# Query weights of later head pairs written between the key matrix' evictions, and the second norm's rows spread by a product with ones

## What is computed

```python
xn = layernorm(ctx, ln1_w, ln1_b)                 # 4 x 77 x 256
ln = layernorm(layernorm(x), ln2_w, ln2_b)        # 4 x 1024 x 256
q, (k, v) = ln @ Wq, split(xn @ Wkv)              # 16 heads of 64
q = q * (1 + f) + f                               # per batch and head
x = x + softmax(q k^T / 8) v @ Wout
y = layernorm(x)
x = x + top2_of_9_experts(y)                      # silu(y Wg) * (y Wu) @ Wd, weighted by the router
```

## Time and profile before

| | us |
|---|---|
| median of 3 runs | 809.99 (809.43 to 810.35) |
| the profiled execution's own time | 810.75 |
| its span, first to last instruction | 809.0 |
| PE busy in the span | 781.2 (97%) |
| DVE, ACT, POOL busy | 662.2, 622.3, 386.2 |
| mean granted TensorE clock | 0.989 |

### The profile page before, as it was taken

The page is one execution under the profiler, slowest core; times in us unless marked ns, Lnnn a source line. Parts: engine busy times, 40 slices in busy tenths (PEclk is TensorE's granted clock), DMA queues, the critical chain, the costliest instruction groups (busy, mean ns, idle before and its releaser), DMA issues.

```text
span 809.0 us, 19727 instructions
## 1 busy us (share of the span) xinstructions
PE 781.2 (97%) x6011; PEld 744.7 (92%) x6011; DVE 662.2 (82%) x1614; ACT 622.3 (77%) x1967; POOL 386.2 (48%) x539
## 2 busy tenths in 40 slices
PE   7998999999999999998999999999999999999994
PEld 7766999999999999897999999999999999999994
DVE  7787798898888887888688988788887878879782
ACT  5878898899899888844677877777787877778772
POOL 3321587688678766771324343332434333233343
PEclk9999999999999999998999999999999999999998
DMA  8375710410410020635475373465656556483222
GB/s 278 116 187 163 224 35 34 144 41 27 148 38 28 34 86 28 212 115 172 102 216 141 51 218 87 104 151 141 182 151 163 146 144 164 90 224 79 47 26 28
DMA packets 78212, 96.40 MB, mean 119 GB/s; under 512 B 10723, under 2 KB 65435, under 8 KB 77979
## 3 DMA queue, kind: packets, MB, share of 16 engines
q1 hardware_dynamic: 64667, 77.25, 31.2%
q0 software_dynamic: 13440, 17.90, 12.6%
HBM read 109.45 MB, written 30.23 MB: 173 GB/s over the span
## 4 chain that ended last, share of the span: by engine, by line
PE 88%; DVE 4%; ACT 2%; issue 2%; POOL 1%; DVEq 1%; DMA 0%; SPq 0%; POOLq 0%; ACTq 0%
PE banks L355 25%; PE banks L356 25%; PE banks L357 25%; PE banks L1471 4%; PE banks L1637 2%; PE banks L1451 2%; PE banks L1485 2%; DVEq L1690 1%; PE banks L1422 1%; PE banks L1434 1%; ACT wq_head L1071 1%; PE banks L1355 1%; ACT prob L1138 1%; PE banks L1609 0%; DVE hid_f L2128 0%
## 5 line engine op out<-in xcount | busy, mean ns | idle before, releaser
L355 PE MATMUL banks<-tok_t_hi,wgt_hi 128*128 128x256 f32 x704 | 201.5, 286 | 3.7 <-issue 2.8
L1015 POOL DMA_INDIRECT result<-res,tok_id x72 | 123.9, 1721 | 164.1 <-ACT res L1273 144.7
L357 PE MATMUL banks<-tok_t_hi,wgt_lo 128*128 128x256 f32 x704 | 197.1, 280 | 0.0
L356 PE MATMUL banks<-tok_t_lo,wgt_hi 128*128 128x256 f32 x704 | 197.0, 280 | 0.0
L1138 ACT ACTIVATE prob<-banks,row_min 128x77 f32<-128x77 f32 x512 | 161.5, 374 | 2.3 <-DVE row_min L1840 2.3
L355 PEld LDWEIGHTS banks<-tok_t_hi,wgt_hi 128*128 128x128 f32 x704 | 133.6, 190 | 5.9 <-issue 5.8
L356 PEld LDWEIGHTS banks<-tok_t_lo,wgt_hi 128*128 128x128 f32 x704 | 133.2, 189 | 0.0
L357 PEld LDWEIGHTS banks<-tok_t_hi,wgt_lo 128*128 128x128 f32 x704 | 133.1, 189 | 0.0
L1138 ACT ACTIVATION_READ_ACCUMULATOR prob<-banks,row_min 128x1 f32 x512 | 130.6, 257 | 0.0
L355 PE MATMUL banks<-wgt_hi,hid_hi 128*128 128x256 f32 x360 | 101.2, 281 | 0.7 <-DVE hid_hi L2156 0.7
L356 PE MATMUL banks<-wgt_lo,hid_hi 128*128 128x256 f32 x360 | 100.8, 280 | 0.0
(11 more groups left out here) (273 smaller groups left out, 2208.6 us busy)
## 6 DMA issues: line engine op xcount, KB each, us to landing
wgt<-in_L_ffn_Wg SPq DMA_DIRECT2D x29, 704.0 KB
wgt<-in_L_ffn_Wu SPq DMA_DIRECT2D x29, 640.0 KB
wgt<-in_L_ffn_Wd SPq DMA_DIRECT2D x29, 640.0 KB
tok<-expert_in SPq DMA_DIRECT2D x32, 258.0 KB, 3.8
spare_wgt<-in_L_ffn_Wg SPq DMA_DIRECT2D x9, 704.0 KB, 4.5
spare_wgt<-in_L_ffn_Wu SPq DMA_DIRECT2D x9, 640.0 KB, 6.1
spare_wgt<-in_L_ffn_Wd SPq DMA_DIRECT2D x9, 640.0 KB, 5.7
valmat_f<-valmat_dram SPq DMA_DIRECT2D x4, 1197.0 KB, 6.3
```

The lines of the kernel that those rows point to most:

```text
L355: nc.tensor.matmul(to, a[0], b[0], start=first, stop=False)
L356: nc.tensor.matmul(to, a[0], b[1], start=False, stop=False)
L357: return nc.tensor.matmul(to, a[1], b[0], start=False, stop=last)
L1015: nc.gpsimd.indirect_dma_start(out, bass.IndirectOffsetOnAxis(ap=tok_id[:, t % NOTES, a:a + 1], axis=0), res[i][:, a, :], None, compute_op ...
```

## The change

Three constants and four places. `FIRST_HEADS = 2`: ACT writes only pairs 0 and 1 before the router's copies; pair m // 4 + 2 follows after the eviction of product m (and the value moves) for m = 1, 5, 9, 13, 17, 21. The wait for all eight pairs becomes one for two pairs and for POOL's scaling. `wq_sb` and `wq_const` get memory that the key matrix doesn't cover. The second norm's rows are loaded into one partition (`ln2_line`), spread by a product with ones into PSUM bank 6, and moved by ACT into `ln2_rows`; their loads stand ahead of those of `wkv`, and PE's first wait includes them. The first run of idle products has 10 in place of 24.

```diff
+FIRST_HEADS = 2
-IDLE = (24, 28)
+IDLE = (10, 28)
@@ loads, on SP
             sp.dma_start(side_row[:], fside.rearrange("b h -> (b h)").unsqueeze(0)).then_inc(small_loaded, 16)
+            for i, v in enumerate((ln2_w, ln2_b)):
+                sp.dma_start(ln2_line[:, i * D:(i + 1) * D], v.unsqueeze(0)).then_inc(small_loaded, 16)
             for i, cols in enumerate(KV_PIECES):
...
-            for i, v in enumerate((ln2_w, ln2_b)):
-                sp.dma_start(ln2_rows[:, i, :], v.unsqueeze(0).to_broadcast([P, D])).then_inc(ln2_loaded, 16)
@@ POOL
-            pool.wait_ge(ln2_loaded, 32)
+            pool.wait_ge(ln2_moved, 1)
@@ ACT
+            act.wait_ge(ln2_spread, 1)
+            nc.scalar.activation(ln2_rows[:].rearrange("p i n -> p (i n)"), bank[6], ACT.Copy).then_inc(ln2_moved, 1)
             round_kv(range(1))
...
-            for c in range(PAIRS // 2):
+            for c in range(FIRST_HEADS):
                 query_head(c)
...
-            for c in range(PAIRS // 2, PAIRS):
-                query_head(c)
-            act.wait_ge(heads_made, PAIRS)
+            act.wait_ge(heads_made, FIRST_HEADS)
+            act.wait_ge(wq_scaled, len(WQ_PARTS))
...
                     if m % 4 == 1:
                         val_move(m)
+                if m % 4 == 1 and m // 4 + FIRST_HEADS < PAIRS:
+                    query_head(m // 4 + FIRST_HEADS)
@@ PE
-            pe.wait_ge(small_loaded, 48)
+            pe.wait_ge(small_loaded, 80)
...
+            nc.tensor.matmul(bank[6], ones[0:1, :], ln2_line[:], start=True, stop=True).then_inc(ln2_spread, 1)
             idle(IDLE[0])
...
+            pe.wait_ge(ln2_moved, 1)
             for c in range(4):
                 turned_keys(c)
```

More of the change, by code:

```diff
@@ L230, in program @@
         wkv_lo = sb("wkv_lo", [P, KT, 2 * INNER], F32R, prep)
-        wq_sb = sb("wq_sb", [P, PAIRS, D], F32, prep)
         wq_gap = sb("wq_gap", [P, PAIRS, D], F32, prep)
         ln2_rows = sb("ln2_rows", [P, 2, D], F32, prep)
-        wq_const = sb("wq_const", [P, PAIRS], F32, prep)
         c_sb = sb("c_sb", [P, CR, D], F32, prep)
@@ L245, in program @@
         k_head = sb("k_head", [P, PAIRS, 2, BM], F32, prep)
+        wq_sb = sb("wq_sb", [P, PAIRS, D], F32, prep)
+        wq_const = sb("wq_const", [P, PAIRS], F32, prep)
         early = ExitStack()
@@ L254, in program @@
         ln_cols = sb("ln_cols", [P, 2, KT], F32, early)
+        ln2_line = sb("ln2_line", [1, 2 * D], F32, early)
         side = sb("side", [P, B, H], F32, early)
@@ L385, in program @@
         ctx_normed = sem("ctx_normed")
-        ln2_loaded = sem("ln2_loaded")
+        ln2_spread = sem("ln2_spread")
+        ln2_moved = sem("ln2_moved")
         ln2_gap_made = sem("ln2_gap_made")
```

## The result

| | before | changed |
|---|---|---|
| median of the runs, us | 809.84 (808.52 to 810.35, 8 runs) | 814.64 (812.75 to 818.19, 8 runs) |
| ratio to before, 95% interval | 1 | 1.0066 (1.0049 to 1.0082) |
| profiled execution, us (span) | 810.75 (809.0) | 814.1 (812.4) |
| mean granted clock | 0.989 | 0.986 |

The account below looks back on a forecast made before the run. PE was taken as the bound, 88% of the span; -1.41 (wait at v2) + 1.37 (stalls) + 0.15 (start) = +0.11 us on a median of 809.99 gave 810.1 us, range for 8 in 10 807.9 to 811.4.

Parts of the forecast that it names:

- part 2: Second norm's rows loaded into one partition and spread by PE at the start: forecast to cost 0.15 us.
- POOL gets its rows some 7 us sooner: In the preparation: POOL has the rows earlier but still starts when wq lands, costed at nothing.
- M31 was to end at 61.1: Sign at the end of the key products: M31 ends as before; wrong if moved over 1 us without a named sign.
- DVE's chain moves by some 0.5: DVE's work from wkv_lo to k_head shifts about 0.5 us, last k_head from 31.53 to 32.0, at no cost.
- M3 not before 33: Named cover for DVE's delay: key product M3 starts no earlier than 33, after the last k_head at 32.0.
- Part 1: Query weights of pairs 2 to 7 moved between ACT's evictions: -1.41 + 0.67 + 0.70 = -0.04 us.
- The wait at v2: PE's stand of 1.41 us before value product v2, forecast to vanish entirely, a gain of 1.41 us.
- the stalls: PE held up before M22 and M26 by the last two pairs on ACT: 0.67 and 0.70 us late.
- Rival (b): No stalls at M22 and M26: 1.37 us less, 808.7 us; chance 0.09.
- PE's start: PE's first wait includes two more small loads, delay taken as 0.1 us; with the product exchange, 0.15 us in all.
- Rival (c): The start costs more: PE's clock rises one stretch of 3.41 us later, 812.0 us; chance 0.10.
- Rival (a): PE's clock isn't halved at 30.6, behind the router's products: 1.6 us less, 808.5 us; chance 0.18.

Follow-up runs that it names:

- heads_alone: Kernel before with only the query weights moved, two pairs ahead and the others between evictions; 810.17 us, ratio 1.0009.
- rows_alone: Changed kernel with all query weights written in their old place, the rows' product with ones kept; 814.23 us, ratio 1.005.
- four_first: pool_waits with four pairs of query weights written ahead in place of two; 809.29 us, ratio 0.9999.
- heads_four: Kernel before with the query weights moved, four pairs ahead of the router's copies, rows loaded as before; 808.56 us, ratio 0.9984.
- pool_waits: Changed kernel with one wait more: POOL's products with wq start only after DVE has made side_shift; 811.3 us, ratio 1.0022.
- heads_four_again: The same kernel as heads_four, run again without any edit; 807.23 us, ratio 0.9976 to the kernel before.
- rows_wait: rows_alone plus the wait of pool_waits (POOL held until DVE has made side_shift); 809.92 us, ratio 1.0002.
- short_products: Changed kernel, no wait added, POOL's first two products with wq cut into eight, one for each pair; 812.55 us, ratio 1.0026.
- wq_later: Changed kernel, no wait added, the loads of wq and wout_t exchanged in SP's order; 811.13 us, ratio 1.002.
- spread_late: four_first with the norm's rows loaded behind wkv, their product just ahead of the keys' products, 24 and 12 idle products; 811.24 us, ratio 1.0017.

## Why the prediction was wrong

- **The step that failed** is in part 2: "POOL gets its rows some 7 us sooner, but starts on `wq` when that lands; at nothing." Two things in it were wrong. I took the landing of `wq` as given, though two reads ahead of it in the same queues were being removed: it came at 14.1, and before at 17.2. And I asked of POOL only who waits for it, and not whom it disturbs. The price was 4.38 us on DVE (of which 0.54 had been there before), 3.05 of wait on PE and 1.45 of clock. With it taken away the kernel measured 811.3 and 811.1, at the top of my range. M31 was to end at 61.1; it ended at 65.2, and none of the rows that I had named as signs says why: the wait for `k_head` isn't among them.
- The trace of before had the sign of it, and I read over it: `side_scale` took 0.73 us at 14.85 and `side_shift`, the same shape, 0.18 at 15.50. POOL's product of the rows, 14.62 to 15.52, lay beside the first of them. In heads_alone that product started at 15.17, behind `side_scale` at 14.63, which took 0.19:

```profile
14.63 0.19 DVE L1736 TENSOR_SCALAR side_scale<-side 128x64 f32<-128x64 f32 x1
...
15.17 0.74 POOL L832 TENSOR_TENSOR ln_rows<-ln_rows 128x256 f32<-128x256 f32 x1 [8.78 <-DMA ln_rows<-in_L_xattn_ln_b]
```

- "DVE's chain moves by some 0.5", with the last `k_head` as the cover: the chain did start 0.7 later. That delay counted: in the changed kernel the last `wkv_lo` started 0.17 behind POOL's product, and in rows_alone, where it started 0.16 ahead of one, it wasn't held. With the chain as early as before it would have been ahead here too (an inference; no run shows it). The cover that I named (M3 not before 33) was the wrong one: with 4.5 us of delay it was PE's fill of the banks behind its 48th product that ran out, at 19.3.
- **Part 1, -0.04 us**: right in each of its terms to 0.16 us. The wait at v2 went; the stalls came at the two places named, at 0.66 and 0.86 against 0.67 and 0.70; heads_alone measured no change (1.0009). Rival (b)'s size, 1.4 us for no stalls, is near what four_first and heads_four show when the stalls are taken away: 2.0 us under pool_waits, and 0.16 to 0.24% under the kernel before.
- **PE's start**: +0.15 forecast, 0.16 at the keys' first product, and the likeness is luck. PE's first instruction came 0.50 late (4.67 for 4.17; I took 0.1), and PE came to the context 0.75 late (8.21 for 7.46; I had 0.27). What made up for it is a clock that rose at 11.76 in place of 13.51, which I had taken as fixed: the stretch of 28 idle products and the context took 0.6 us less. The rise isn't set by the kernel alone: one and the same kernel has it at 13.73 in the profile of heads_four and at 8.73 in that of heads_four_again, and so its first product of the keys at 12.43 and at 10.87. Rival (c), a clock that rises 3.4 us later, didn't come. The second small load, issued at 3.00 and used at 4.67, took 1.67 us at most, against 1.78 for `side_row` before. The Trainium skill, "DMA: Bandwidth & Descriptors", section "Anatomy of one DMA — SWDGE (gpsimd) path", gives 2.0 us for loads that GpSimd issues; these are SP's. By that figure PE would have started near 5.0, and the trace is under it.
- **Rival (a)**, a clock not halved behind the router's products: in none of the twelve profiled executions of this study. It is halved for 3.41 us in six and for 6.83 us in six.
- No rival had the cause. The one on the slow side closest in kind was (c), on PE itself; a collision of two other engines over a tile that arrives sooner wasn't among them.

**What stays open.** Part 2 without the collision seems to cost something beside the moved weights, and nothing beside the old order: pool_waits less heads_alone is 1.1 us and four_first less heads_four 0.7 (1.2 by the ratios, and 1.9 against heads_four_again), while rows_wait less the kernel before is 0.4 (0.2 by the ratio). In profiles the clock behind the router's products is halved for 3.41 us with the rows loaded as before (four of four), and for 6.83 where they are spread by the product and PE doesn't wait for `k_head` (five of five of pool_waits, four_first, rows_wait, short_products, wq_later). In rows_wait that would be covered by PE's old wait before v2, and indeed that wait is gone there. The mean clock over all runs points the same way: 0.9895 for heads_four both times, 0.9883 to 0.9888 before, 0.9874 to 0.9881 for pool_waits, wq_later, rows_wait and four_first. That mean also has another source in it: near 374 to 380 us the clock is halved a second time, for 3.41 us in the profiles of heads_four, rows_wait and spread_late and for 6.83 in the other nine, the second profile of the very kernel of heads_four among them. It is not shown what in part 2 would set it, and no run was made for it.

## What to carry to other kernels

When a change makes data land sooner, or removes a load that stood ahead of others in a queue, ask of every engine that will now start earlier whom it will run beside, VectorE and GpSimd above all: a GpSimd product of 2.4 us held a VectorE instruction of 0.19 us for 2.2. An instruction that takes several times as long as its twin of the same shape is the sign to look for in the trace of before. And work that is moved between evictions is free only as long as each stretch has room for it: the same move is worth nothing with two pairs ahead and 0.2% with four.

## What was new about the hardware

- VectorE and GpSimd take turns by whole instructions, in both directions: `wkv_lo` 1.22 us alone and 3.42 beside a product of GpSimd, `side_scale` 0.19 and 2.37, and GpSimd's product 2.4 alone and 3.36 behind `wkv_lo`. VectorE's `k_head`, which reads one operand from the banks and one from SBUF, is not held: 0.47 us at 20.30, with GpSimd busy from 20.14, as everywhere.
- A row of 1 KB read into 128 partitions, twice, stands ahead of a 1 MB load that takes 10.5 us from issue to landing, and 8.3 without them, though the two move only 256 KB. In spread_late the same two rows are read at the same place in SP's order, ahead of `wq`, but into one partition, and `wq` takes 7.9 us. So it is the reading into 128 partitions, not the two loads as such, that goes with the longer time.
- While PE stood for 3.05 us (changed kernel) the clock fell to half for 3.41 us, near the end of a stand of 1.62 us (spread_late) for 6.83 us, and not at all at stands of 0.7 us (rows_alone) and of 1.41 and 1.46 us (ahead of v2, before and in rows_alone). The time at which the clock first rose went from 7.65 to 13.73 us over the twelve profiled executions, with PE's first work at 4.1 to 4.8 in all of them; 8.73 in the profile of heads_four_again and 13.73 in that of heads_four, the same kernel.
